# One program for preparation and edge pass: the barrier removed, the left-over sums moved into the pass's first steps

## The reference, cut to what matters

```python
h = relu(layernorm(x))                          # node rows, 128 wide
msg_input = concatenate([h[src], h[dst], edge_attr])
m = relu(msg_input @ W1.T + b1)                 # one message per edge
agg = segment_sum(m @ W2.T + b2, dst)           # sum over each node's edges
upd = relu(agg @ Wu.T + bu)
y = layernorm(h + upd) * gamma + beta
x1 = x + y
...
deg = segment_sum(edge_weight, dst)             # used by the last layers
A = counts of edges (dst, src)                  # dense, for the later layers' sums
```

## Time and profile before

| | us |
|---|---|
| median of 3 runs (1937.61 to 1939.03) | 1938.01 |
| span of the profiled execution | 2170.3 |
| preparation, start to POOL's first row gather | 75.8 |
| first row gather to the end of the 20 | 32.9 |
| end of the 20 to POOL's first gather of the pass | 21.9 |
| POOL's gathers in the pass, first to last | 1215 |
| last gather to the end of the program | 824 |

### The profile page before, as it was taken

One profiled execution on the slowest core, in us unless ns is written; L12 is line 12 of the kernel. 1 busy time (PEld: TensorE's weight loads), 2 busy tenths in 40 slices (PEclk: granted clock), 3 DMA queues, 4 the chain that ended last, 5 costly groups with the idle time before them and its releaser, 6 DMA issues. The chain is left out here.

```text
span 2170.3 us, 30067 instructions
## 1 busy us (share of the span) xinstructions
PE 1378.5 (64%) x9130; PEld 904.1 (42%) x9130; DVE 1129.6 (52%) x3500; ACT 812.2 (37%) x3272; POOL 841.7 (39%) x877
## 2 busy tenths in 40 slices
PE   3235444445445454545545445799899999899997
PEld 2123233333333333333333333356656666455444
DVE  7756666667667666666666666431442224311101
ACT  2235455555545555454545544111343432100000
POOL 5636666666666666666666665000000000000001
PEclk8566766666666666666665666899999999899999
DMA  6444434434443433434434443103100001871770
GB/s 198 143 96 116 115 113 116 122 115 121 121 116 112 122 120 114 118 113 122 119 112 117 120 119 103 30 12 139 34 29 1 10 7 39 305 266 65 264 293 29
DMA packets 200853, 245.67 MB, mean 113 GB/s; under 512 B 36794, under 2 KB 174053, under 8 KB 200674
## 3 DMA queue, kind: packets, MB, share of 16 engines
q1 hardware_dynamic: 142978, 137.56, 20.1%
q0 software_dynamic: 29472, 65.73, 11.7%
q10 hardware_dynamic: 28224, 40.15, 5.2%
HBM read 174.00 MB, written 55.93 MB: 106 GB/s over the span
## 5 line engine op out<-in xcount | busy, mean ns | idle before, releaser
L989 POOL DMA_INDIRECT arena<-dram_PHL,src_of x786 | 765.2, 974 | 472.1 <-remote 205.4
L1327 PE MATMUL psum<-arena 128*128 128x150 f16 x1568 | 238.9, 294 | 604.3 <-DVE aw_out L1034 330.4
L1327 PEld LDWEIGHTS psum<-arena 128*128 128x128 f16 x1568 | 153.4, 125 | 762.2 <-issue 380.6
L1228 ACT ACTIVATE arena<-psum 128x512 f16<-128x512 f32 x202 | 121.9, 603 | 429.3 <-remote 294.5
L1236 ACT ACTIVATE arena<-psum 128x150 fp8e4<-128x150 f32 (+1 forms) x588 | 173.6, 295 | 181.4 <-remote 93.8
L1241 ACT ACTIVATE arena<-psum,arena 128x150 f16<-128x150 f32 (+1 forms) x588 | 228.6, 389 | 1.6 <-remote 1.6
L1309 PE MATMUL psum<-arena 128*128 128x128 f16 x1612 | 182.2, 281 | 39.0 <-DMA arena<-dram_QHL 36.3
L1054 DVE SCALAR_TENSOR_TENSOR agg_all<-psum,agg_all 128x64 f32<-128x64 f32 x202 | 43.8, 217 | 283.4 <-remote 281.4
L1314 PE MATMUL psum<-arena 128*128 128x512 f16 x404 | 184.5, 552 | 3.6 <-issue 3.6
L1244 ACT ACTIVATE aw_out<-psum 128x150 f32<-128x150 f32 (+1 forms) x588 | 179.6, 305 | 0.0
L1043 DVE SCALAR_TENSOR_TENSOR arena<-psum,arena 128x512 f16<-128x512 f32 x202 | 137.9, 683 | 76.2 <-issue 41.3
(11 more groups left out here) (344 smaller groups left out, 2080.3 us busy)
## 6 DMA issues: line engine op xcount, KB each, us to landing
dram_aw<-aw_out ACTq DMA_DIRECT2D x196, 200.0 KB
arena<-dram_aw SPq DMA_DIRECT2D x6, 6400.0 KB
arena<-dram_aw SPq DMA_DIRECT2D x3, 4800.0 KB
arena<-in_ea_quads SPq DMA_DIRECT2D x51, 256.0 KB
arena<-dram_rel SPq DMA_DIRECT2D x51, 256.0 KB
arena<-arena SPq DMA_DIRECT2D x408, 32.0 KB
arena<-dram_PHL,src_of POOLq DMA_INDIRECT x806
arena<-dram_aw SPq DMA_DIRECT2D x2, 4000.0 KB
```

Source lines behind the costliest of these rows:

```text
L989: nc.gpsimd.indirect_dma_start(gathered_p[:, slot, k, :], None, d["PHL"], bass.IndirectOffsetOnAxis(ap=src_of[:, b:b + 1], axis=0)).then_i ...
L1327: done = nc.tensor.matmul(thirds[:, :, i * PKEY:(i + 1) * PKEY], hot_lo[:, u, p, :], hot_key[:, u, p], start=True, stop=True)
```

## The change

The preparation's instructions and the pass's stand in one block of each engine. What it does:

1. The two barriers and the semaphore clearing between them are gone. The pass starts on each engine behind that engine's own last work of the preparation, and waits on semaphores of the preparation where it reads its results.
2. `degrees`, `out_of_bands`, `reach` and `badness` leave DVE's preparation. They are cut into pieces (`left_over`) that stand at the end of DVE's steps 0 to 4, 10 to 16 and 17 to 21.
3. The degrees are turned on PE (step 5), copied out by DVE (step 5) and stored by SP in rows of 256 numbers (step 4 of SP's order); the weights are folded in step 8 (`FOLD`) and not in step 2.
4. The buffers of P and Q groups are used in turn by threes. `row_fields` has one multiply-subtract on `past` and one addition in the place of a subtraction and a multiply-add on the key. ACT copies `rel_of`. The weight sums on PE come before the field transposes.
5. The gathers of all groups stand in one loop, with the ring of five slots (`AHEAD_P = 0`, so no slot is added).

```diff
-        prepare(nc, new, d)
-        end_phase()
-        edge_pass(nc, new, d)
+        prepared = prepare(nc, new, d)
+        edge_pass(nc, new, d, prepared)
...
-            n, k = len(tiles_of(c)), c % 2
+            n, k = len(tiles_of(c)), c % 3
-                if c >= 2:
-                    dve.wait_ge(pq_stored[k], 48 * (c // 2))
+            if c >= 3:
+                dve.wait_ge(pq_stored[k], 48 * (c // 3))
...
-                    step(nc.vector.tensor_scalar(rows[:, :, :, A_KEY], rows[:, :, :, A_KEY], base[:, 0:1], None,
-                                                 ALU.subtract))
-                    step(nc.vector.scalar_tensor_tensor(out=rows[:, :, :, A_KEY], in0=past[:, :, :], scalar=OUTSIDE,
-                                                        in1=rows[:, :, :, A_KEY], op0=ALU.mult, op1=ALU.add))
+            step(nc.vector.tensor_scalar(past, past, OUTSIDE, base[:, 0:1], ALU.mult, ALU.subtract))
+            dve.wait_ge(pair_rows, 16 * PCOLS)
+            step(nc.vector.tensor_tensor(rows[:, :, :, A_KEY], rows[:, :, :, A_KEY], past, ALU.add))
...
                 def gather(g):
-                    slot = g % NPG
-                    if g >= NPG:
-                        pool.wait_ge(pre, g - NPG + 1)
+                    if g == SLOTS_P:
+                        pool.wait_ge(d["h_stored"], 16 * G)
+                    if SLOTS_P + AHEAD_P <= g < 2 * SLOTS_P + AHEAD_P:
+                        pool.wait_ge(pre, g - SLOTS_P - AHEAD_P + 1)
+                    elif g >= 2 * SLOTS_P + AHEAD_P:
+                        pool.wait_ge(pre, g - SLOTS_P + 1)
...
-                for g in range(NPG, MG):
+                for g in range(MG):
                     gather(g)
...
+                def left_over(s):
+                    if s == 0:
+                        weights_of_rows()
+                    if s == 1:
+                        count_of_first()
+                    if s == 2:
+                        weight_of_first()
+                    if s == 3:
+                        weights_of_both()
+                    if s == DEGREES:
+                        degrees_of_rows()
+                    if s == DEGREES + 1:
+                        degrees_out()
+                    if s in (10, 11):
+                        out_of_band(s - 10)
+                    if s == 12:
+                        most_of_weights()
+                    if s == 13:
+                        reach_of_weights()
+                    if s == 14:
+                        bad_order()
+                    if s in (15, 16):
+                        bad_weights(s - 15)
+                    if 17 <= s < 17 + PARTS_OF_ROW:
+                        sum_bad(s - 17)
+                    if s == 17 + PARTS_OF_ROW:
+                        sum_all_bad()
...
+        DEGREES, FOLD = 4, 8
...
-                    if s == 4:
+                    if s == FOLD:
                         load_nodes(0)
                         load_nodes(1)
...
+                    if s == DEGREES:
+                        store_degrees()
```

More of the change, by code:

```diff
@@ L145 @@
 SLOTS_P, BANDS_HELD = 5, 8
+AHEAD_P = 0
+ROW_T = NCOL // 2
+KEPT = 256
 def share_buffers(nc, d):
@@ new lines, in gathered_of, with strip @@
+def gathered_of(d, g):
+    if SLOTS_P <= g < SLOTS_P + AHEAD_P:
+        return d["gathered_ahead"][g - SLOTS_P], 16 * blocks_of(g)
+    before = [k for k in range(g % SLOTS_P, g + 1, SLOTS_P) if not SLOTS_P <= k < SLOTS_P + AHEAD_P]
+    return d["gathered"][g % SLOTS_P], 16 * sum(blocks_of(k) for k in before)
+def strip(d, row, rows, at, shape, dt):
+    size = 4 if dt in (F32, I32) else 2
+    flat = d["arena"][:, :, :].rearrange("p t n -> p (t n)")[0:shape[0], 0:NT * ROW_T]
+    if dt is not F16:
+        flat = flat.bitcast(dt)
+    view = flat.rearrange("p (t n) -> p t n", t=NT)[:, row:row + rows, at // size:at // size + math.prod(shape[1:])]
+    assert at % size == 0 and at + math.prod(shape[1:]) * size <= 2 * ROW_T
+    axes = [f"a{i}" for i in range(len(shape) - 1)]
+    sizes = {a: n for a, n in zip(axes[1:], shape[2:])}
+    return view.rearrange(f"p t ({' '.join(axes)}) -> p t {' '.join(axes)}", **sizes)
@@ L997, in _ @@
             def _(dve):
+                prepare_vector(dve)
                 def hots(g):
@@ L1162, in raise_flag, with linked @@
                     step(nc.vector.tensor_copy(d["flag"][:, :], row[:, 7:8]))
+                rows, past, w_slot, w_half, sums = d["rows"], d["past"], d["w_slot"], d["w_half"], d["sums"]
+                out_sum, norms, most, reach = d["out_sum"], d["norms"], d["most"], d["reach"]
+                per_dst, bad, bad_rows = d["per_dst"], d["bad"], d["bad_rows"]
+                left = [0]
+                def linked(ins):
+                    left[0] += 1
+                    ins.then_inc(left_step, 1)
+                    dve.wait_ge(left_step, left[0])
@@ new lines, in most_of_weights @@
+                def most_of_weights():
+                    dve.wait_ge(d["w_rooted"], 1)
+                    dve.wait_ge(d["w_in"], 64)
+                    b1 = d["b1_rows"]
+                    for a in range(3):
+                        nc.vector.reduce_max(most[:, a:a + 1], norms[:, a * D:(a + 1) * D], axis=AX.X)
+                    linked(nc.vector.scalar_tensor_tensor(out=norms[:, 3 * D:4 * D], in0=b1, scalar=-1.0, in1=b1,
+                                                          op0=ALU.mult, op1=ALU.max))
+                    linked(nc.vector.reduce_max(most[:, 3:4], norms[:, 3 * D:4 * D], axis=AX.X))
@@ new lines, in reach_of_weights, with bad_order @@
+                def reach_of_weights():
+                    linked(nc.vector.tensor_tensor(most[:, 0:1], most[:, 0:1], most[:, 1:2], ALU.add))
+                    linked(nc.vector.scalar_tensor_tensor(out=reach[:, 0:1], in0=most[:, 0:1], scalar=float(D) ** 0.5,
+                                                          in1=most[:, 3:4], op0=ALU.mult, op1=ALU.add))
+                    linked(nc.vector.tensor_copy(reach[:, 1:2], most[:, 2:3]))
+                def bad_order():
+                    nc.vector.tensor_tensor(bad[:, :, 0], d["nxt_i"], d["dst_i"], ALU.is_lt)
@@ L1164, in _ @@
+                dve.wait_ge(d["agg_cleared"], 6)
+                dve.wait_ge(d["rel_of_ready"], 2)
+                dve.wait_ge(d["field_act"], len(range(0, PCOLS, 2)))
+                dve.wait_ge(d["field_dve"], len(range(1, PCOLS, 2)))
                 nc.vector.memset(last[:, :], 0.0).then_inc(cleared, 1)
@@ L1311, in build @@
                                              stop=False)
-                    pe.wait_ge(gathered[g % NPG], 16 * sum(blocks_of(k) for k in range(g % NPG, g + 1, NPG)))
+                    pe.wait_ge(*gathered_of(d, g))
                     for part in range(2):
-                        done = nc.tensor.matmul(out, ident_h[:, :], gathered_p[:, g % NPG, 0:n, part * D:(part + 1) * D],
+                        done = nc.tensor.matmul(out, ident_h[:, :], slot_of(d, g)[:, 0:n, part * D:(part + 1) * D],
                                                 start=False, stop=(part == 1))
```

1148 lines of the change are left out of this document (589 added, 559 removed).

## The result

The changed kernel takes **1907.64 us** (median of 4 runs, 1905.24 to 1909.69) against 1938.52 (4 runs, 1937.61 to 1941.23) on the same chip: a ratio of 0.9838, 95% interval 0.9824 to 0.9852, or 30.9 us less. The forecast was 1920.5, range 1907 to 1935. The direction and the bound of the pass were right, the size was not: the saving was 30.9 us against 17.5. It is also near the case "all bounds good" (1908), but that is a coincidence: that case had 7.0 us at the start of the chain and 18.1 at the barrier, and the traces show 0.7 and 23.4.

A forecast was written before the change was run, and what follows sets the result against it. The prediction took POOL's chain of gathers as the bound of ordinary runs, with DVE close behind. Savings of 29.6 us less 8.3 lost gave 21.3, corrected to 17.5 us: 1938.0 - 17.5 = 1920.5 us, range 1907 to 1935.

The forecast's parts named there:

- all bounds good: Every term at its favourable bound: 7.0 + 4.9 + 18.1 = 30 us saved, giving 1908 us.
- the start of the chain: First gather, waiting for the last store of PHL, comes earlier: 2.5 us saved, bounds 0 to 7.0.
- the barrier: POOL's 21.92 us wait between gathers 20 and 21 goes, first group built at 92 (88 to 98): 21.9 us saved, 18.1 corrected.
- The correction of 3.8 us: DVE's 3.78 us wait at the last field copy taken as absent from ordinary runs, so their hole is 18.1, not 21.9.
- 14 to 18 us of the 824 shrink: Last gather to the end, 824.3 us: 14 to 18 us are PE's four groups behind POOL, shrinking when POOL is the bound.
- The 20 gathers: POOL's first 20 gathers: 1.9 us saved beside the row fields (0 to 4.9), and 3.3 beside left-over sums leave here.
- Left-over work in the steps: DVE's 22 us of moved work and waits in steps 5 to 10: POOL loses 0 to 10 us, taken as 4.
- The cover: First group built at 92, POOL's 20th gather ending at 101: 9 us before POOL would wait.
- Stretching in the pass: Gathers of the pass lengthened: 3.3 us by left-over sums and 1 by the two-input check, lost.
- Consumers as the bound: Rival, 0.20: the pass goes at the pace of DVE and PE; 8.7 us saved, 1929 us.
- Shift eaten: Rival, 0.12: POOL's hole at the barrier fills with other waits, and waits in steps 5 to 10 take the rest; 1937 us.
- Slower: Rival, 0.08: free-running POOL meets DVE's two-input instructions anywhere, doubling the pass's 23 us of gather stretching; 1943 us.

The follow-up runs named there:

- the ordinary execution of before: The kernel before, unchanged, run again for a trace of an execution without the pauses of PE: 1936.5 us, span 1935.0 us.

## What held the barrier

The hole was 23.7 us and not 18.1. The correction of 3.8 us assumed that DVE, once its wait of the earlier trace rows is gone, would let the barrier go earlier. DVE was indeed earlier, but the barrier was not. The instructions of the sequencers at the end of the first program, by the view of its line, in the ordinary execution of before (durations in ns, then the start):

```profile
L284 POOLq DRAIN  x1: 28279/28279/28279, 89.2 to 89.2; - x1
...
L284 SPq DRAIN  x1: 384/384/384, 107.2 to 107.2; - x1
L284 DVEq DRAIN  x1: 178/178/178, 111.5 to 111.5; - x1
```

DVE is at the barrier at 111.7. POOL's drain ends at 89.2 + 28.3 = 117.5, which is 10.2 us behind the end of its 20th gather (107.2), and SP's first load of the pass follows at 119.0. In the execution that the forecast was read from, the same drain took 21.8 us and ended at 112.5, ahead of DVE's 117.2, so there DVE was last. In the two executions without pauses that have this end of the program (the other is the one with a memset, below) POOL's drain was, at 117.5 and 116.9.

Why did it take 10.2 us? SP issued the stores of the degrees, which write single values, at 103.9 to 107.1, beside the last gathers. In the execution that the forecast was read from it issued them at 109.4 to 111.9, behind the end of the 20th gather (108.7), and there the drain ended 3.8 us behind that gather. The next run moved these stores behind the barrier.

```diff
 # SP, end of the preparation
-                for q, row in enumerate((0, 3)):
-                    sp.dma_start(d["deg"][row, 0:whole * PAIR * P] ...
 # SP, start of the pass
                 load_bands(0)
+                for q, row in enumerate((0, 3)):
+                    sp.dma_start(d["deg"][row, 0:whole * PAIR * P] ...
                 load_rel(1)
```

> The kernel before with its four stores of degrees, which write single values, moved behind the barrier, to SP's place between the bands of the first groups and the second load of rel; nothing else. In ordinary executions of the kernel before, DVE is at the barrier at 111.7 and POOL's drain ends only at 117.5, 10.2 us behind its 20th gather and 5.8 behind the last row's landing, where it ends 3.8 us behind the 20th gather in the kernel with the barrier alone, which has no such stores there. Theory (the small packets of these stores hold the last rows and with them POOL's drain): the drain ends near 111, DVE at 111.7 is last at the barrier, the hole shrinks from 23.7 to about 18 us and the time from 1937 to 1932, unless SP's next loads, now behind the stores, make POOL wait in the first steps for as much. Rival (the drain is long for another reason): drain still near 117, 1937 or more.

It took 1941.13 us (11 runs), a ratio of 1.0016 (1.0007 to 1.0025). The drain, and POOL's gathers that waited:

```profile
L284 POOLq DRAIN  x1: 21887/21887/21887, 90.3 to 90.3; - x1
```

```profile
126.65 0.94 POOL L988 DMA_INDIRECT arena<-dram_PHL,src_of  x1 [18.29 <-PE psum L1313]
...
146.89 0.94 POOL L988 DMA_INDIRECT arena<-dram_PHL,src_of  x1 [5.19 <-PE psum L1313]
...
157.00 0.94 POOL L988 DMA_INDIRECT arena<-dram_PHL,src_of  x1 [5.44 <-PE psum L1313]
```

The drain ends at 112.2, 3.8 us behind the 20th gather, and the hole is 18.3 us: the theory's numbers. The stores held the drain; by which way is not shown. The gain of 5.4 us was lost again, and more, by what the expectation warned of: SP's wait for the slow stores (from 130.5 to 136.8) now stood ahead of its next loads, and POOL waited 10.6 us in the first steps. The changed kernel turns the degrees on PE, so that their stores write whole rows, and puts them in step 4, where neither happens.

## The barrier alone, the left-over work alone, the buffers alone

**The barrier.** The changed kernel, cut into two programs behind POOL's first 20 gathers. The left-over work stays in the steps. The clearing of the semaphores is not put back; with it the barriers of the kernel before took 1.5 us (117.5 to 119.0).

```diff
+        with nc.Block() as block:      # prepare_*, and on POOL gathers of groups 0 to 4
+            ...
+        nc.all_engine_barrier()
+        nc.all_engine_barrier()
         with nc.Block() as block:
             @block.sync
             def _(sp):
-                prepare_sync(sp)
```

> The changed kernel with the barrier put back behind the first 20 gathers, and nothing else: the left-over work stays in the steps. Theory (the hole was made of the barrier and of what SP and DVE may only do behind it): POOL ends its 20 gathers at 102, barrier 1.7, 11.9 from SP's first load to POOL's release, so a hole of 13.6 us and 1907.6 + 13.6 = 1921. Rival (the hole was DVE's left-over work): 1908 to 1912.

1932.19 us (6 runs), a ratio of 0.9957 (0.9942 to 0.9972) to before: by the ratios the barrier costs 23 us of the 30.9. In the traces the chain ends 22.3 us later. POOL at its hole:

```profile
97.73 0.94 POOL L896 DMA_INDIRECT arena<-dram_PHL,src_of  x1 [0.30 <-issue]
116.58 0.94 POOL L896 DMA_INDIRECT arena<-dram_PHL,src_of  x1 [17.91 <-PE psum L1462]
```

and the first rows of SP and PE behind it, in their views by time:

```profile
103.41 0.50 SPq L938 DMA_DIRECT2D arena<-dram_rel  x1
104.35 5.20 SPq L948 DMA_DIRECT2D arena<-arena  x8
109.59 2.51 SPq L956 DMA_DIRECT2D arena<-dram_QHL  x4
```

```profile
113.95 1.01 PE L1457 MATMUL psum<-arena 128*128 128x128 f16 x8 [33.40 <-DMA arena<-dram_QHL]
```

The hole of 17.9 us is 3.8 of drain, 0.9 of the barriers' semaphores (102.5 to 103.4), 10.5 from SP's first load to PE's first build, and 2.6 to POOL's release. The expectation of 13.6 missed the drain. The rest of the 22.3 us is a consequence that I had not named. POOL waits 4.1 us more ahead of its 69th and 101st gather, and the gathers of the pass are stretched by 3.8 us more, against 3.5 less in the first 20. I put the waits down to left-over work that meets consumers with no lead. That is argued: it fits that the kernel before has the barrier, no left-over work in the steps and no such waits, but the two kernels differ in more than that.

**The left-over work** in one piece ahead of the first one-hot rows, without a barrier:

```diff
                 nc.vector.memset(last[:, :], 0.0).then_inc(cleared, 1)
+                for s in range(18 + PARTS_OF_ROW):
+                    if s != DEGREES + 1:
+                        left_over(s)
                 hold_rows()
```

> The changed kernel with the left-over work of DVE (all but the copy of the turned degrees) in one piece ahead of the pass's first one-hot rows, without a barrier. Theory: the first one-hot rows move from 82.9 to about 104, the first build to 108, POOL's release to 109.5, against an end of its 20 gathers at 102: a hole of 7 us, and the steps lose their left-over work at no gain: 1907.6 + 7 = 1915. Rival (moving the work costs the steps as much as it saves ahead of them): 1908 or less.

1914.28 us (4 runs), a ratio of 0.9870 (0.9847 to 0.9893), with a hole as expected:

```profile
111.19 0.94 POOL L1006 DMA_INDIRECT arena<-dram_PHL,src_of  x1 [7.68 <-PE psum L1449]
```

The 23 us of DVE work (84.4 to 107.6 in its trace) cost 6.6 us when they stand ahead of the pass, and nothing in the steps but their stretching of gathers.

**The third buffer:** in the preparation `c % 3` and the waits that go with it back to `c % 2`.

> The changed kernel with the buffers of products and halves by twos, as before. Theory (the third buffer starts the chain 2.2 us earlier, and the chain carries that to the end): 1907.6 + 2.2 = 1910, first gather near 75.8. If SP's full queue set the start of the chain and not the buffer, 1908 and a first gather near 73.7; if DVE's later row fields meet the first three gathers again as well, up to 1913.

1912.07 us (4 runs), a ratio of 0.9864 (0.9844 to 0.9885), so 4 to 5 us by the medians. The traces give 3.1 us: the chain starts only 0.9 us later (74.53), but its first gather then meets the long instruction of the row fields. POOL and DVE, both of this kernel:

```profile
74.53 4.42 POOL L1006 DMA_INDIRECT arena<-dram_PHL,src_of  x1 [5.16 <-DMA dram_PHL<-arena]
```

```profile
74.48 3.82 DVE L537 TENSOR_TENSOR arena<-arena 128x1664 f16<-128x1664 f16 x1
```

In the changed kernel the same instruction starts at 70.05 and ends at 73.88, and the first gather starts at 73.66. With two buffers DVE stands 3.42 us at group 5 for a store of Q again, which is the wait that the prediction wanted to remove, and its row fields come 4.4 us later. But the last store of PHL is issued only 0.9 us later (70.89 against 70.03). So of what the buffer is worth here, 3.0 us are stretch, as it shifts DVE's row fields to the other side of the chain's start; the 0.9 us of start are no more than runs without this edit differ by.

## Is POOL the bound, and how much does the ring cover?

**One and four memsets on POOL ahead of each group of gathers**, 197 times, first with one memset of 64 values a partition in either kernel, then with four of 16 values in the changed one:

```diff
                     if g >= SLOTS_P:
+                        pool.wait_ge(extra_done, 4 * (g - SLOTS_P))
+                        for part in range(4):
+                            nc.gpsimd.memset(extra[:, part * 16:(part + 1) * 16], 0.0).then_inc(extra_done, 1)
```

> The changed kernel with one more small instruction on POOL, a memset of 64 values a partition, ahead of each group of gathers from the 6th on, 197 in all. Theory (POOL's chain bounds the pass of the changed kernel): the time grows by 197 times what one memset and the gap behind it take in its trace; I guess 0.4 to 0.6 us a group, 80 to 120 us in all, so 1990 to 2030. Rival (the consumers are the bound): the first 0.9 us a group are free (5.0 us a step of POOL against 4.1 of DVE), so 1908 to 1915.

> The kernel before with the same memset ahead of each of the 197 groups of gathers of its pass. Theory (POOL's chain bounds it in ordinary executions too): it grows by as much as the changed kernel does, 80 to 120 us. Rival (its pass is held by the consumers, or by pauses of PE): by less than half as much.

> The changed kernel with four memsets of 16 values a partition on POOL ahead of each of 197 groups of gathers. With one memset a group the chain grew by only 23 to 36 ns a group, as the memset filled the gap of 0.30 us that stands behind a gather; so one memset hardly loaded POOL. Theory (POOL bounds the pass): three of the four lie outside the gap, at 0.1 to 0.2 us each, so the time grows by 60 to 120 us, and by as much as the group's pace in the trace grows times 197. Rival (the consumers are the bound, with 0.9 us a step to spare): under 15 us.

The changed kernel went to 1915.35 us (ratio 0.9882, 0.9866 to 0.9899) with one memset and to 1935.44 (10 runs, ratio 0.9989, 0.9979 to 0.9999) with four; the kernel before to 1942.04 (ratio 1.0029, 1.0013 to 1.0044) with one. My guess at the price of a memset was far too high. With one a group (changed kernel):

```profile
301.41 1.30 POOL L1010 DMA_INDIRECT arena<-dram_PHL,src_of  x1 [0.31 <-issue]
302.71 0.17 POOL L1007 MEMSET extra<- 128x64 f32 x1
303.04 0.95 POOL L1010 DMA_INDIRECT arena<-dram_PHL,src_of  x1 [0.16 <-POOL extra L1007]
```

The memset and its gap take 0.33 us where the gap alone was 0.30. So what counts is what the chain grew by, from the 21st gather to the last, against the same kernel without it: 7.1 us in the changed kernel (times: 8.5 by the ratios), 4.5 us in the one before (5.6), and with four memsets 26.8 us (29.3). All three grow by about as much as the chain, in both kernels: POOL's chain is the bound of the pass before and after. Had the consumers been the bound, these runs would have cost nothing. The four memsets are the strong case; in the kernel before, the growth of 5.6 us has an interval of 2.5 to 8.5, and that POOL never waits behind the hole in the unedited kernel's ordinary trace says more.

**One more instruction on DVE in each of the 202 steps**, a maximum over 512 values, 0.678 us each, 137 us in all:

```diff
                     left_over(s)
+                    if s < MG:
+                        dve.wait_ge(extra_done, s)
+                        nc.vector.reduce_max(extra[:, :], ..., axis=AX.X).then_inc(extra_done, 1)
```

> The changed kernel with one more instruction on DVE in each of the 202 steps, a maximum over 512 values of a partition, 0.5 to 0.7 us each and 100 to 140 us in all. Theory (POOL bounds the pass): it disappears in DVE's idle time but for what the ring can't cover near groups 12 and 21, where slots come free only 10.2 and 4.9 us ahead of their use: 1908 to 1918. Rival (DVE bounds it): 2010 to 2050.

1916.24 us (4 runs), a ratio of 0.9891 (0.9874 to 0.9907): 9 to 10 of the 137 us are paid (by the medians or by the ratios). POOL's rows with a wait of over 1 us (a fourth, at 236.81, waited 0.76):

```profile
184.52 0.94 POOL L1007 DMA_INDIRECT arena<-dram_PHL,src_of  x1 [2.14 <-PE psum L1450]
...
210.51 0.94 POOL L1007 DMA_INDIRECT arena<-dram_PHL,src_of  x1 [6.24 <-PE psum L1450]
...
216.40 0.94 POOL L1007 DMA_INDIRECT arena<-dram_PHL,src_of  x1 [1.06 <-PE psum L1450]
```

They lie where the ring has least to spare. In the changed kernel PE's build of group 21, which releases a slot, and the gather of group 26 that reuses it stand like this, each in the view of its engine:

```profile
203.60 1.06 PE L1445 MATMUL psum<-arena 128*128 128x512 f16 x2
```

```profile
209.60 0.94 POOL L1006 DMA_INDIRECT arena<-dram_PHL,src_of  x1 [0.30 <-issue]
```

Released at 204.66, used at 209.60: 4.9 us to spare, the least of all groups. At groups 0 to 11, with the left-over work, it is 11.6 to 18.0 us.

**Three slots** in place of five (`SLOTS_P = 3`):

> The changed kernel with a ring of three slots of gathered rows in place of five. A slot of the changed kernel is released 11 to 18 us ahead of its reuse in the steps with left-over work and 4.9 us ahead at the tightest, group 21. Two slots less take 2 x 5.02 = 10.0 us off that. Theory: the ring runs empty near groups 12 to 25 for 5.1 us in all, besides up to 2 for the way of the rows; 1912.7, range 1911 to 1917. Also the first build must be ready 10 us earlier, at 92, and is at 88.6. Rival (a fuller ring has hidden more than this, as in before, where POOL waited in the pass): 1925 or more.

1913.72 us (4 runs), a ratio of 0.9884 (0.9867 to 0.9900). POOL waits, beside the gaps of 0.3 us, 5.5 us in four places, ahead of groups 15, 19, 23 and 24, against 5.1 worked out from the slack, and its chain ends 4.5 us later. The times grew by 6.1 us by the medians and 8.9 by the ratios. So the slack read from two rows tells about what a smaller ring costs. Five slots leave 4.9 us at the tightest group, a little less than one group's 5.0; no run has four.

## Two tries at an earlier start

The last store of PHL is issued at 70.03 though its halves are ready at 66.2, as SP is still issuing the stores of P, Q and h0 of earlier groups. First, these stores of groups 4 to 6 move behind the last stores of PHL and QHL:

```diff
-            sp.dma_start(group_ap(d["P"], c), pq[:, k, 0:n, 0]).then_inc(pq_stored[k], 16)
-            sp.dma_start(group_ap(d["Q"], c), pq[:, k, 0:n, 1]).then_inc(pq_stored[k], 16)
-            sp.dma_start(group_ap(d["h0"], c), x[:, t]).then_inc(h_stored, 16)
+            if c < G - 3:
+                store_rest(c)
+        for c in range(G - 3, G):
+            store_rest(c)
```

> The changed kernel with the stores of P, Q and h0 of groups 4, 5 and 6 moved behind the stores of PHL and QHL of group 6 in SP's queue; nothing else. In the changed kernel DVE has the last halves at 66.2, but SP issues their store at 70.03, since it is still issuing earlier ones. Theory (SP's queue sets the start of the chain, not the buffer): last PHL store issued near 66.5, first gather at 70; but the row fields' 3.83 us instruction (70.05 to 73.88) then meets the first gathers and gives up to 3 us back: 1904 to 1907 against 1907.6. Rival (the DMA engines are full, so that an earlier issue lands no earlier): first gather at 73 or later, 1907 to 1908.

1907.39 us (5 runs), a ratio of 0.9846 (0.9832 to 0.9859). The start is where it was expected, and so is what takes it back:

```profile
69.98 0.96 POOL L1014 DMA_INDIRECT arena<-dram_PHL,src_of  x1 [4.92 <-DMA dram_PHL<-arena]
71.25 3.34 POOL L1014 DMA_INDIRECT arena<-dram_PHL,src_of  x1 [0.30 <-issue]
74.90 0.95 POOL L1014 DMA_INDIRECT arena<-dram_PHL,src_of  x1 [0.30 <-issue]
```

In the traces the chain ends 2.3 us earlier; the times don't tell it from the changed kernel. The second try also moved the stores of h0 further back, and reordered DVE:

```diff
         add_bias(4)
+        row_lengths()
         low_parts(4)
         add_bias(5)
+        add_bias(6)
+        row_slots()
         low_parts(5)
         low_weights()
-        add_bias(6)
-        row_lengths()
         low_parts(6)
```

> A version meant to beat the changed kernel: the stores as in the experiment beside it, h0 of groups 4 to 6 even behind the loads for the first built groups, and on DVE the row lengths, the bias of group 6 and the comparison of slots with lengths in idle stretches ahead of the low halves of group 5, so that the last halves are ready near 64. Theory (the start of the chain is carried one for one to the end): first gather at 67.5 to 69, up to 3 us of stretching by the row fields' long instruction, the 20th gather ends at 97 to 99 in place of 101.9, and the ring, with 4.9 us of slack at group 21, holds: 1903 to 1905. Rival (the ring runs empty because the consumers start no earlier): gain under 2 us, 1906 to 1908.

1908.70 us (5 runs), a ratio of 0.9849 (0.9835 to 0.9863), no gain. The reason is one row of DVE:

```profile
63.13 0.56 DVE L520 TENSOR_TENSOR arena<-psum,arena 128x384 f32<-128x384 f32 x1 [3.45 <-DMA dram_Q<-arena]
```

The bias of group 6, moved ahead, waits for its buffer's earlier store, and the low halves of group 5 that I put behind it wait with it. The last halves came at 68 and not at 64, the first gather at 71.07 with 3.62 us. This try shows nothing of the theory behind it. No version that measurably beats the changed kernel was found.

## Why the prediction was right, and where not

- **The bound.** Right, though it rested on a sum and not on a row: the ordinary trace and the memsets show POOL's chain as the bound of both kernels. The check "14 to 18 us of the 824 shrink" gave 812.0, a shrinking of 12.3. The traces account for 9.4 of the 13.4 us by which the forecast was short: 5.3 at the barrier, 4.2 in POOL's waits and 2.7 in the stretching of the pass, less 1.8 at the start, 0.5 in the first 20 gathers and 0.5 behind the last one. So misses of both signs met in the sum.
- **Start of the chain.** Forecast 2.5, measured 0.7. The last store of PHL was issued at 70.03, inside the 2 to 7 us ahead of 73.6. But the ordinary execution of before had issued it at 72.08, and its rows landed sooner (2.2 against 3.6 us behind the issue). The prediction's reading of DVE's wait at group 5 was right (the run with two buffers), and so was the caution that little of it would reach the start. Of its two reasons the order of the stores in SP's queue is shown: with other stores moved behind it, the last store of PHL is issued at 66.25 and the chain starts at 69.98. That the DMA engines were full is not borne out, as the lag of 3.7 us from issue to start stayed.
- **The 20 gathers.** Forecast 5.2 with what leaves, measured 4.7. The part beside the row fields, of which 1.9 was taken, went wholly, and that hid the left-over work's 3.3 us, which came back within these 20 and not behind them: a later row field or an earlier gather brings it back (the runs with two buffers and with early stores). The prediction counts four long left-over instructions with two inputs; its rows have three (L528, L531, L533), so its 7.5 us should be 5.6.
- **The barrier.** The first build was at 86.7, the release at 88.6; the bounds were 88 to 98, taken as 92, so it came 1.3 us ahead of the lower one. The wait before the 21st gather is gone, as said. The step that failed is the correction of 3.8 us: it took DVE for the last at the barrier in ordinary runs, and POOL's own drain was. The hole was 23.7 us and not 18.1.
- **Left-over work in the steps.** Single steps lost ground on POOL, two of them (8.4 and 7.3 us) above all, but the ring never ran empty: forecast 4 us of waits, measured none. The term was mis-sized twice. The cover, taken as 9 us, was 13.6 at the first slot, as the first build came 5 us before the value I took. And the steps lost less than I priced: I had 6.7 us a step against POOL's 5.1, 8 us in five steps, but the builds of groups 0 to 5 end 26.3 us apart, 5.3 a step, and the gathers that reuse their slots start 26.6 apart, as the same sums stretch them. The lead was still 13.9 us at group 5, and 11.6 at the least in groups 0 to 11. The waits that I priced at the fold were there and reached nobody who counts: ACT stood 8.25 us for attributes at 146.05 and PE 6.30 us at 149.60, both over the bound of 6 us that I gave, at a place where a slot was 10 us or more early.
- **Stretching in the pass.** Forecast 4.3 lost, 1.6 measured for the 786 gathers behind the 20th, with part of the left-over work's stretch in the first 20, where the table has it. POOL's mean gather is 964 ns, inside 960 to 985. The gathers beside left-over sums took 2.62, 2.60, 1.30 and 1.77 us, two of them over the 1.6 to 2.3 that I gave.
- **The rivals.** Consumers as the bound: ruled out by the memsets. Shift eaten: no. Slower, by a free-running stretch of 22 ns a gather: the gathers of the pass were not stretched twice as much (12.3 against 10.7 us).

## What to carry to other kernels

Before pricing a change to a stretch between two programs, ask of each engine when its drain ends, and not only when its last instruction does: an engine that has issued DMAs can be the last at a barrier with nothing on its own row. When one engine issues an unbroken chain behind a ring, what the others do costs nothing but what it stretches that engine's own instructions by, as long as the slot is released before it is wanted; read that slack from two rows per group, and trust the smallest. Where a profiled execution is far above the median, take a second one before working out sums from it.

## What the runs showed of the hardware

- A gather that starts during a long DVE instruction with two inputs in SBUF ends only 0.8 to 1.0 us behind it. In the changed kernel the gather at 90.09 took 2.62 us and ended at 92.71, against L1194 on DVE (89.84 to 91.72), and the one at 98.00 ended at 100.60 against L1199 (97.90 to 99.79). A gather that had started first is not stretched: in the ordinary execution of before the one at 90.41 took 0.94 us beside L528, which started at 90.75. The Trainium skill, "SBUF — State Buffer", section "SBUF: two separate sides", says that such a DVE instruction and a GpSimd one that reads SBUF, as a gather reads its indices, hold the shared ports by turns, each for a whole instruction; the trace agrees for the gathers. The same section infers that a `tensor_tensor` does not hold up the writing of a DMA's descriptors; here both of these are `tensor_tensor`, and the gathers beside them waited.
- DVE is not seen to pay for it. The row fields' instruction on 128x1664 values took 3.82 us where no gather ran beside it but for its last 0.04 us (the run with the barrier, 70.22), where one started behind it (two buffers, 74.48), and where one had started ahead of it (early stores: gather at 69.98, DVE at 70.14).
- An instruction with one input can hold a gather too, but not each does. In the ordinary execution of before the gather of 76.58 took 2.15 us and ended 0.6 us behind L521 (75.85 to 78.10), which has one tensor as its input; the gather of 94.00 began during the reduction L530 (93.61 to 95.50) and took 0.94. That L521 took 2.25 us and the instruction in its place in the changed kernel 0.69 (69.33) shows nothing of ports: the first works on every fourth value of the rows, the second on values that lie side by side.
- POOL's 0.30 us behind a gather is not lost to other instructions: a memset of 0.17 us fits into it and makes a group longer by 0.02 to 0.04 us.
- A drain on POOL ended 3.8 us behind the last gather in three executions, and 9.7 and 10.2 us behind it where stores of single values were issued beside the last gathers (3,264 packets of SP's queue between 104 and 112 us). What a drain waits for is not shown.
- The same program was once profiled at 2170.3 us, with 130 gathers in 200 us and a wait of 281.4 us on DVE without a releaser, and later at 1935.0 with 159 and none of that. The cause of those pauses stays open.
